# A three-stage transformer kernel: another slot order, smaller tiles and half-size broadcasts in its cross-attention

## The reference, cut to what matters

```
xn = _ln(x, lnx_g, lnx_b)            # 256 x 128
yn = _ln(y, lny_g, lny_b)            # 64 x 64, the context
q = jnp.einsum('bsc,hcd->bhsd', xn, wq)
k = jnp.einsum('btc,hcd->bhtd', yn, wk)
v = jnp.einsum('btc,hcd->bhtd', yn, wv)
a = jax.nn.softmax(jnp.einsum('bhsd,bhtd->bhst', q, k) * D ** (-0.5), axis=-1)
o = jnp.einsum('bhst,bhtd->bhsd', a, v)
x_out = x + o @ li1_w + li1_b
```

## Time and profile before

| what | us |
|---|---|
| median of 3 runs | 1399.13 (1396.72 to 1405.87) |
| the profiled execution | 1397.05 |
| its span | 1395.2 |
| TensorE busy | 1307.3 (94% of the span) |
| VectorE busy | 980.1 (70%) |
| ScalarE busy | 853.1 (61%) |
| GpSimd busy | 663.5 (48%) |
| mean granted TensorE clock | 0.973 |

### The profile page before, as it was taken

The page is one execution under the profiler, slowest core; times in us unless marked ns, Lnnn a source line. Parts: engine busy times, 40 slices in busy tenths (PEclk is TensorE's granted clock), DMA queues, the critical chain, the costliest instruction groups (busy, mean ns, idle before and its releaser), DMA issues.

```text
span 1395.2 us, 44119 instructions
## 1 busy us (share of the span) xinstructions
PE 1307.3 (94%) x18510; PEld 850.3 (61%) x18510; DVE 980.1 (70%) x2242; ACT 853.1 (61%) x1349; POOL 663.5 (48%) x1139
## 2 busy tenths in 40 slices
PE   7899999998999998989999999998989999999895
PEld 4455555554455553556777777665767777677584
DVE  6788888875555554577888888754567887787343
ACT  3687777776656665567777777654446666542352
POOL 4455666532001003245766666452337777445265
PEclk6999999998999998999999999999999999999998
DMA  7000000000600000000000001002001111122451
GB/s 230 4 4 3 4 3 3 3 4 2 174 0 1 1 1 1 1 2 18 33 26 26 33 18 33 33 33 61 1 17 48 48 48 48 47 83 90 145 169 45
DMA packets 54884, 53.85 MB, mean 39 GB/s; under 512 B 8999, under 2 KB 48939, under 8 KB 54432
## 3 DMA queue, kind: packets, MB, share of 16 engines
q1 hardware_dynamic: 50784, 44.21, 10.4%
q0 software_dynamic: 2816, 6.11, 1.3%
q10 hardware_dynamic: 1088, 0.72, 0.3%
HBM read 20.35 MB, written 14.49 MB: 25 GB/s over the span
## 4 chain that ended last, share of the span: by engine, by line
PE 77%; DVE 11%; POOL 4%; ACT 3%; issue 3%; DMA 1%; SPq 1%; POOLq 0%; DVEq 0%; ACTq 0%
PE psum L1574 6%; PE psum L1602 4%; DVE a_nm L623 4%; PE psum L960 4%; PE psum L962 4%; PE psum L961 4%; PE psum L1234 4%; PE psum L1198 3%; PE psum L2641 3%; PE psum L381 2%; PE psum L535 2%; PE psum L1545 2%; PE psum L1586 2%; PE psum L2062 2%; PE psum L2071 2%
## 5 line engine op out<-in xcount | busy, mean ns | idle before, releaser
L1657 DVE TENSOR_REDUCE b_nm<-psum 128x4 f16<-128x1024 f32 x128 | 156.6, 1223 | 52.2 <-PE psum L1579 51.5
L740 ACT ACTIVATE a_prob<-psum 128x768 f32<-128x768 f32 (+1 forms) x160 | 136.1, 853 | 50.5 <-PE psum L467 48.8
L623 DVE TENSOR_REDUCE a_nm<-psum 128x4 f16<-128x1024 f32 (+1 forms) x96 | 117.3, 1222 | 26.3 <-PE psum L480 25.1
L792 POOL TENSOR_SCALAR_AFFINE_SELECT a_prob<-a_prob 128x512 f32<-128x512 f32 x128 | 84.3, 659 | 106.4 <-ACT a_prob L740 106.3
L171 POOL TENSOR_TENSOR f_ln_rstd<-f_ln_tmp,pow_half 128x4 f32<-128x4 f32 x24 | 25.4, 1058 | 199.6 <-DVE f_ln_tmp L160 199.5
L1088 ACT ACTIVATE xo_sb<-psum,f_w_h_s 128x512 f32<-128x512 f32 x64 | 44.0, 688 | 88.3 <-PE psum L962 88.3
L1574 PE MATMUL psum<-b_QTh,b_KTh 32*128 32x256 f16 x512 | 70.4, 273 | 7.3 <-DVE b_nm L1657 5.2
L1579 PE MATMUL psum<-b_KTh,b_QTh 32*128 32x256 f16 x512 | 70.7, 273 | 1.2 <-DVE b_nm L1657 1.2
L1574 PE MATMUL psum<-b_QTh,b_KTl 32*128 32x256 f16 x512 | 69.4, 268 | 0.0
L1574 PE MATMUL psum<-b_QTl,b_KTh 32*128 32x256 f16 x512 | 69.3, 268 | 0.0
L1579 PE MATMUL psum<-b_KTl,b_QTh 32*128 32x256 f16 x512 | 69.3, 268 | 0.0
(11 more groups left out here) (462 smaller groups left out, 4623.2 us busy)
## 6 DMA issues: line engine op xcount, KB each, us to landing
f_h_wh<-b_rden SPq DMA_DIRECT2D x64, 128.0 KB, 2.1
f_h_wh<-c_rden SPq DMA_DIRECT2D x64, 128.0 KB, 2.1
expert_in<-empty SPq DMA_DIRECT2D x8, 662.5 KB, 11.4
m_xt<-expert_in SPq DMA_DIRECT2D x7, 662.5 KB, 4.9
m_w<-in_L_ffn_w_dram SPq DMA_DIRECT2D x16, 256.0 KB
x_sb<-in_x_dram SPq DMA_DIRECT2D x8, 256.0 KB, 4.5
f_w_h_w<-in_L_ffn_h_w_dram SPq DMA_DIRECT2D x2, 1024.0 KB, 7.7
out_dram<-m_send SPq DMA_DIRECT2D x8, 256.0 KB, 2.4
```

What stands on the lines that cost most here:

```text
L623: nc.vector.tensor_reduce(out, psum[:, banks, :].rearrange("p i (a b) -> p i a b", a=groups), X, ALU.max, negate=True).then_inc(max_done, 1)
L740: nc.scalar.activation(prob[unit % 5][:, :, 0:width], psum[:, first:first + 2, 0:width], ACT.Exp, scale=SCALE).then_inc(exp_done, 1)
L792: nc.gpsimd.affine_select(out=diagonal, in_=diagonal, compare_op=ALU.is_ge, fill=0.0, base=0, pattern=[[0, 4], [1, P]], channel_multiplier ...
L1657: v.tensor_reduce(self.nm[:, :, :].rearrange("p t (j r) -> p j t r", r=32)[:, 2 * e:2 * e + 2, :, g], self.pr.psum[:, 2:4, :].rearrange("p ...
```

## The change

- **Order.** New slots. Both score groups stand in a row (slots 0 and 1), values at 2 and 4, the maxima of the next batch at 3 (behind the second exponential, which still reads the banks), then `o`, `nm`, `k`, `q0`, `q1`. On VectorE `rden` moves to slot 5 and `vector_scaled` to slot 9. ScalarE drains the values before the projections.
- **Maxima** are made from the high halves alone: 32 products instead of 96.
- **Values** use 64 x 32 tiles: for each e eight products, one for each of 4 head positions and each half of the keys, into two banks (4 and 5). The weight tile holds no zeros any more. One activation copies V.
- **Sums** are made once per batch, 16 products with 128 x 32 tiles and 128 columns each, into columns 256 to 383 of bank 4. They come out as 128 x 128, so the reciprocal has 128 elements per partition instead of 256.
- **Broadcast**: 8 DMAs per batch of 64 KB each instead of 4 of 128 KB.
- `k` and `v` have their halves padded to 128 rows with zeros.
- `tensor_values` of batch n at e = 0 still waits for `rden` of n - 1. `vector_rden` waits for `num_out` too, since it reads the bank that ScalarE reads.
- **Router bias**: its weights are loaded in the stage before (class `Gate`), and GpSimd prepares the rows at the start of the last feed-forward.
- The rows of `li1_w` are reordered outside the kernel to fit the new order of heads.

```diff
-    SLOT = {"z": -11, "k": -8, "q0": -7, "q1": -6, "v": -4, "nm": -1, "o": 14}
-    SCORES, VALUES, MAXIMA = {0: 0, 1: 2}, {0: 3, 1: 5}, -4
-    FIRST, LAST = -23, 8 * (B - 1) + 17
+    SLOT = {"v": -7, "z": -13, "o": 13, "nm": -2, "k": -10, "q0": -9, "q1": -9}
+    COPIED = {**SLOT, "v": -6}
+    SCORES, VALUES, MAXIMA, FIRST_MAXIMA = {0: 0, 1: 1}, {0: 2, 1: 4}, -5, -4
+    BANKS = (4, 5)
+    FIRST, LAST = -25, 8 * (B - 1) + 17
...
             for i in range(2):
-                for (x, y) in ((0, 0), (0, 1), (1, 0)):
-                    for j in range(4):
...
+                for j in range(4):
...
-        for i in range(2):
-            for pair in range(2):
-                g = 2 * e + i
-                t.matmul(psum[TC * pair:TC * pair + TC, 6, 0:T], self.group_col[:, g, :, :].rearrange("p a d -> p (a d)"),
-                         prob[:, pair, i * T:i * T + T], start=(g == 0), stop=(g == self.G - 1), skip_group_check=True)
...
+        for b in range(4):
+            for a in range(2):
+                keys = slice(TC * a, TC * a + TC)
+                inst = t.matmul(psum[D * b:D * b + D, self.BANKS[a], 0:T], self.V[n % 2][keys, 2 * (2 * e + b % 2) + b // 2, :],
+                                prob[keys, b // 2, b % 2 * T:b % 2 * T + T], start=True, stop=True, skip_group_check=True)
+        if e == 1:
+            inst = self.tensor_sums(n)
         inst.then_inc(self.av_done, 1)
+
+    def tensor_sums(self, n):
+
+        for e in range(2):
+            prob = self.prob[(2 * n + e) % 3]
+            for h in range(2):
+                for b in range(4):
+                    first = b % 2 * T + h * P
+                    inst = self.nc.tensor.matmul(self.pr.psum[self.D * b:self.D * b + self.D, self.BANKS[0], T:T + P],
+                                                 self.chosen[:, e, h, :], prob[:, b // 2, first:first + P], start=False,
+                                                 stop=(e + h == 2), skip_group_check=True)
+        return inst
...
         if n:
-            v.wait_ge(self.rb_there, 64 * n)
-        v.reciprocal(self.rden[:, :], self.pr.psum[:, 6, 0:T]).then_inc(self.rden_done, 1)
+            v.wait_ge(self.rb_there, 128 * n)
+        v.wait_ge(self.num_out, 2 * (n + 1))
+        v.reciprocal(self.rden[:, :], self.pr.psum[:, self.BANKS[0], T:T + P]).then_inc(self.rden_done, 1)
...
     def vector_slot(self, s):
-        for _, n in self.parts(s, {0: self.MAXIMA}):
+        for n in self.maxima_at(s):
             self.vector_max(n)
         for use in self.parts(s, self.SLOT):
             if use[0][0] in "qk":
                 self.vector_low(use)
-        for _, n in self.parts(s, {0: 6}):
+        for _, n in self.parts(s, {0: 5}):
             self.vector_rden(n)
-        for _, n in self.parts(s, {0: 11}):
+        for _, n in self.parts(s, {0: 9}):
             self.vector_scaled(n)
...
-        for k, n in self.parts(s, {4: -13, 0: -23, 1: -21, 2: -18, 3: -16}):
+        for k, n in self.parts(s, {4: -18, 0: -25, 1: -23, 2: -20, 3: -20}):
             self.vector_normed(n, k)
...
     def gpsimd_slot(self, s):
-        for _, n in self.parts(s, {0: -11}):
+        for _, n in self.parts(s, {0: -13}):
             self.gpsimd_low(n)
+        for _, n in self.parts(s, {0: -24}):
+            self.ln_in.gpsimd_rstd(n)
         for _, n in self.parts(s, {0: -22}):
-            self.ln_in.gpsimd_rstd(n)
-        for _, n in self.parts(s, {0: -20}):
             self.gpsimd_unnormed(n)
-        for _, n in self.parts(s, {0: -17}):
+        for _, n in self.parts(s, {0: -19}):
             self.ln_c.gpsimd_rstd(n)
-        for _, n in self.parts(s, {0: -15}):
             self.ln_x.gpsimd_rstd(n)
-        for _, n in self.parts(s, {0: 16}):
+        for _, n in self.parts(s, {0: 15}):
             self.gpsimd_output(n)
...
             for g in range(self.G):
-                y.dma_start(self.rb[:, g, :], self.rden[g:P:4, :].unsqueeze(1).to_broadcast([P // 4, 4, T])).then_inc(
-                    self.rb_there, 16)
+                for h in range(2):
+                    y.dma_start(self.rb[:, g, h * P:h * P + P],
+                                self.rden[2 * g + h:P:8, :].unsqueeze(1).to_broadcast([P // 8, 8, P])).then_inc(self.rb_there, 16)
...
-            if n == 2 and routing:
-                routing.gpsimd_bias()
...
+                    gate.start()
...
+        self.gate.gpsimd_halves()
```

More of the change, by code:

```diff
@@ L1884, in __init__ @@
         self.zi = sb("zi", [P, 2, C])
[L1885 to L1888, removed]
+        self.zT, self.cT = ([sb(f"{x}T{k}", [P, cols], F32 if k == "w" else F16) for k in "whl"]
+                            for x, cols in (("z", T), ("c", P)))
+        self.halves = {x: [sb(f"{x}{half}", [P, HID], F16) for half in "hl"] for x in ("wq", "wk", "wv")}
         self.QT = [[sb(f"QT{half}{i}", [P, G, T], F16) for half in "hl"] for i in H2]
         self.KT = [[sb(f"KT{half}{i}", [P, G, TC], F16) for half in "hl"] for i in H2]
-        self.V = [sb(f"V{i}", [P, H // 2, 2, self.D]) for i in H2]
+        self.V = [sb(f"V{i}", [P, H // 2, self.D]) for i in H2]
         self.nm = sb("nm", [P, 2, P], F16)
@@ L1921, in bank_of @@
     def bank_of(self, use):
-        return self.pr.psum[:, (5, 7)[self.ring.slot(use)], :]
+        return self.pr.psum[:, (6, 7)[self.ring.slot(use)], :]
     def tokens(self, m, n):
@@ L1928, in row2, with maxima_at @@
         return self.w[name][:, :].unsqueeze(1).to_broadcast([P, 2, C])
+    def maxima_at(self, s):
+        if s == self.FIRST_MAXIMA:
+            return [0]
+        return [n for _, n in self.parts(s, {0: self.MAXIMA}) if n]
     def vector_prepare(self):
-        v, G, done = self.nc.vector, self.G, self.prepared
+        v, G, done, low = self.nc.vector, self.G, self.prepared, slice(CC, P)
         v.memset(self.nm[:, :, :], 0.0)
-        for m in self.V:
-            v.memset(m[...], 0.0)
-        v.memset(self.group_col[...], 0.0).then_inc(done, 1)
+        for m in (*self.cT[1:3], *self.halves["wk"], *self.halves["wv"]):
+            v.memset(m[low, :], 0.0)
+        v.memset(self.chosen[...], 0.0).then_inc(done, 1)
         v.tensor_reduce(self.group[:, :], self.pr.ident[:, :].rearrange("p (j r) -> p r j", r=32)[:, 0:G, :], X,
@@ L1951, in gpsimd_split @@
             self.w.arrived(g)
-        g.tensor_copy(high[:, :], self.w[x][:, :]).then_inc(self.split_high, 1)
+        rows = slice(0, P if x == "wq" else CC)
+        g.tensor_copy(high[rows, :], self.w[x][:, :]).then_inc(self.split_high, 1)
         g.wait_ge(self.split_high, i + 1)
-        g.tensor_tensor(low[:, :], self.w[x][:, :], high[:, :], ALU.subtract).then_inc(self.split_low, 1)
+        g.tensor_tensor(low[rows, :], self.w[x][:, :], high[rows, :], ALU.subtract).then_inc(self.split_low, 1)
     def tensor_drained(self, use):
@@ L2218, in scalar_slot @@
             self.scalar_scores(n, e)
[L2219 removed]
+        for e, n in self.parts(s, self.VALUES):
+            self.scalar_values(n, e)
+        for use in self.parts(s, self.COPIED):
             self.scalar_projection(use)
[L2221 to L2222 removed]
     def gpsimd_unnormed(self, n):
@@ L2237, in gpsimd_low @@
             g.wait_ge(self.pro_full, self.ring.full(("v", n - 1)))
-        for whole, high, low in (self.cT, self.zT):
-            inst = g.tensor_tensor(low[:, :], whole[:, :], high[:, :], ALU.subtract)
+        for (whole, high, low), rows in ((self.cT, slice(0, CC)), (self.zT, slice(0, P))):
+            inst = g.tensor_tensor(low[rows, :], whole[rows, :], high[rows, :], ALU.subtract)
         inst.then_inc(self.z_low, 1)
@@ L2859, in layout @@
             a[k] = np.ascontiguousarray(v.reshape(*v.shape[:-1], 4, 4, -1).swapaxes(-3, -2).reshape(v.shape))
+        elif k == "L1_xattn_a2_li1_w":
+            heads = [(2 * e + b % 2) * 4 + 2 * (b // 2) + i for e in range(2) for i in range(2) for b in range(4)]
+            a[k] = by_chunk(v.reshape(H, -1, C)[heads].reshape(v.shape))
         elif k.endswith(("li1_w", "li3_w", "li2_b")):
```

104 lines of the change are left out of this document (51 added, 53 removed).

## The result

The changed kernel takes 1422.64 us (median of 4 runs, 1421.41 to 1429.44), the kernel before 1397.93 beside it: ratio 1.0191 [1.0159, 1.0224]. The forecast was 1413 in 1385 to 1430. The direction and the mechanism came out; the loss is 25 us where the sum said 14.4. The profiled execution is 1421.97 us, its span 1420.2, 25.0 more than before.

| part | before | after | measured | predicted |
|---|---|---|---|---|
| up to the first reciprocal's end | 1034.0 | 1031.9 | -2.1 | -0.5 |
| 15 turns | 175.7 | 201.2 | **+25.5** | +15.8 |
| from the last reciprocal's end | 185.5 | 187.1 | +1.6 | -0.9 |

What follows compares the result with a forecast made beforehand. PE bounds the kernel before; after, VectorE's reciprocal-broadcast-scaling loop binds. Turns of 182.8 plus long issues 8.7 make 191.5 (+15.8); head -0.5, tail +0.6, router bias -1.5 give +14.4, said as 1413 us, range 1385 to 1430.

Steps and rivals of the forecast that it cites:

- PE's demand: PE's own work per cross-attention batch, claimed to fall from 11.7 to about 9.4 us.
- The loop binds: VectorE's loop from reciprocal through broadcast, scaling and maxima to the next reciprocal sets the batch: 12.6 us against 11.74.
- rival B: The loop binds but long issues are rare or hidden: 12.6 us per batch, 1405 us; chance 0.28.
- 6.62 us from the reciprocal to the scaling: Broadcast term of the loop: 4.04 us now plus 2.58 for four more DMA issues on SyncE.
- 5.98 from the scaling to the next reciprocal: VectorE's rest of the loop: scaling 1.14, `zi` 0.52, maxima 2.26, statistics 0.39 and 0.76, reciprocal 0.91 us.
- Long issues, +0.58: Instruction loads starting inside SyncE's burst of eight broadcasts lengthen an issue: 0.58 us more per batch, 13.2 in all.
- the landing: Time from a broadcast DMA's issue to its landing, 2.1 us, left unchanged within the broadcast term.
- Head: The part up to the first reciprocal's end: -0.5 us, with 2 either way.
- Tail: After the last reciprocal: +0.6 us for the feed-forward starting behind `o` of batch 14, -1.5 for the router bias wait.
- Rival C: PE, idle in lumps, drops to half clock; 14 us a batch, 1425 us; chance 0.1.
- Rival A: The broadcast does not bind: 11.2 us a batch with long issues, 1383 us, or 1370 at the floor; chance 0.22.
- So PE sets the pace: Kernel before, cross-attention: PE busy 11.73 of 11.74 us a batch, VectorE and GpSimd close behind.

Runs made afterwards that it cites:

- run 1: The changed kernel with four of its eight broadcast DMAs per batch left out, so the output differs; 1384.06 us, ratio 0.99 to the kernel before.
- run 2: The kernel before with each of its four broadcasts per batch cut into two of 64 KB, nothing else changed; 1429.35 us, ratio 1.0248.
- run 4: The changed kernel with VectorE's scaling two slots later (11 for 9), behind the maxima; 1433.54 us, ratio 1.0205 to the kernel before.
- Run 8: The kernel before with the maxima made from the high halves alone (32 products a batch instead of 96); 1405.83 us, ratio 0.9999.
- run 9: The changed kernel with five of eight broadcasts on SyncE and three on ScalarE; 1408.93 us, ratio 1.003 to the kernel before.
- run 5: The changed kernel with six broadcasts on SyncE, two on ScalarE: 1404.12 us, ratio 1.0002; with the scaling two slots later as well: 1434.01 us, 1.0206.
- run 7: The changed kernel, scaling two slots later, `o` behind k, statistics for `zi` earlier: 1410.25 us, 1.0017; also with six/two broadcasts on SyncE/ScalarE: 1411.16 us, 1.0047.

## Why the prediction was right, and where its sum was short

- **PE's demand** (9.4 us): close. Values 0.66 for 0.6, sums 1.08 for 1.0, maxima 0.41 for 0.37; at full clock PE is busy for 9.75 to 9.77 us in five turns and for 10.27 in three (as in the turn shown above). It had no weight while the loop stood at 12.6.
- **The loop binds**: right, in 15 of 15 turns, with 57.8 us of waiting for the DMA, and runs 1 and 2 show it from both sides. The forecast's mechanism holds, and rival B (few long issues) is out with 13 of them. That 1% is about what a measurement tells from no change was too cautious: the interval here is 0.3% to either side.
- **6.62 us from the reciprocal to the scaling**: 6.50 undisturbed. The 2.58 for four more issues fits (5.03 for 2.46). From the last issue's end to the scaling it takes 1.44 with 64 KB and 1.55 with 128. By the cost that the Trainium skill, "DMA: Bandwidth & Descriptors", section Anatomy of one DMA, gives for GpSimd's path, that difference would be 0.15, an estimate, and the trace, of SyncE's DMAs, comes near it (0.11).
- **5.98 from the scaling to the next reciprocal**: 5.85.
- **Long issues, +0.58**: 0.61. Right.
- **The term that failed is the landing.** "From issue to landing 2.1 us, of which I leave all" took the median as if it were constant. It is 2.0 without an instruction load behind the last issue, and about 2.9 to 3.8 with one: +0.84 a turn, 12.6 us. With -1.8 and -1.6 from the first two terms above and +0.5 from the long issues that makes the 9.7 by which the turns exceed 191.5. That the total came within the forecast's own 1404 to 1424 is in part luck: without the two terms that were too long the turns would have missed by 13.1. I also took loads as evenly spread. Of 25, 20 start between the first issue and the scaling, in 59% of the time. PE, which runs k, q, the scores and the values just then and idles before the scaling, consumes its instructions there; that this is the reason was argued, not tested.
- **Head**: -2.1 for -0.5, inside the 2 either way.
- **Tail**: +1.6 for -0.9. The first feed-forward's transposes start 1.6 us after the last reciprocal, as foreseen behind `o` of batch 14; but this `o` took 3.51 us, not 1.95. PE's timeline, with the router's first wait, and the busy time of the stretch of `o`:

```profile
1231.35 3.51 PE L2019 MATMUL psum<-c_w_li,f_h_wl 128*128 128x128 f32 x16 [4.47 <-DVE f_h_wl L2169]
1234.70 0.60 PE L1220 MATMUL psum<-ident,b_w_wq 128*128 128x128 f32 x4
...
1262.18 0.18 PE L2552 MATMUL psum<-m_hot,m_earlier 128*128 128x32 f16 x1 [0.68 <-DVE m_carry L2500]
```
```profile
1231.10:1234.50 3.40, 3.15 (x15) 3.18 (x16) 3.27 (x15) 0.00 (x0) 0.00 (x0) 0.50 0.03 9
```

  After 4.47 us without work PE ran at 0.50, the 1.2 GHz level, 1.6 us more than the same product took before. The wait of 1.46 us for the router's bias is gone, but 4 us later PE now waits 0.68 us for VectorE, where it did not before, and of the 1.5 forecast some 0.8 are gained. These two make 2.3 of the 2.5 us by which the tail is over.
- **Rival C**, the clock: it exists (0.95 over the stage, five stretches of 3.4 us at half clock in it) and costs nothing in the turns, since the loop has no product in it: 5.85 stays in those batches too. In this kernel it costs only where nothing hides it, 1.6 in the tail; in run 4, where `o` is in the loop, it costs in the turns too.
- **Rival A**: not what happened, but its price was near. For a broadcast of 4.8 us it had 11.2 a turn and 1383 us, 16 below the kernel before; run 1, with 4.76, has 10.9 and is 12 below. By the Trainium skill, "TensorEngine Tiling (Array Packing)", section PSUM Bottleneck, the copies out of PSUM may be next. With the broadcast halved VectorE leads the chain that ended last (its maxima, which it reads from PSUM, have 20.9%), but 23% of it are still broadcast, and a turn is 10.7 us where VectorE's own chain was put at 10.3. Run 1, 1062 to 1170 us:

```profile
by line: DVE c_nm L2132 20.9%; DMA f_h_wh<-c_rden 14.3%; issue 9.1%; SPq L2289 8.6%; DVE c_z L188 5.5%; DVE c_zi L188 4.9%; DVE c_QTl L2145 4.4%; DVE c_rden L2161 4.4%; POOL c_lni_rstd L171 4.4%; POOL c_lnx_rstd L171 2.9%; POOL c_lni_tmp L1
```

- **"So PE sets the pace" before**: read too strongly. Run 8 cuts PE by 0.7 us a batch and gains nothing, and in the trace of before the scaling already waits for the DMA in 10 of 15 turns, 0.16 to 1.51 us. It changed nothing in this sum, because the loop I added was longer than both.

## What to carry to other kernels

When a change halves an engine's work by splitting a transfer, count issues, not bytes: eight DMAs of 64 KB cost 2.6 us more than four of 128 KB, and they stood in a loop in which nothing could hide them. Price a DMA in a loop by its distribution, not by its median: the one late landing in the trace of before was a sample of the term that this sum missed. And before moving an instruction out of one loop, follow who stands behind it on the other engines; the later scaling took 2.2 us out of its own loop and made another of 13.7, which moving `o` behind k only shortened.

## What the hardware showed that was not expected

- Loads of instructions for PE (16 KB, 0.9 to 1.6 us, one per 8 us of this stage) disturb a broadcast in both halves of its life: one issue takes up to 1.85 us instead of 0.60, or the landing is 0.9 to 1.8 us late. That the late packets stand behind the load on their DMA engine is likely, not shown.
- Issues on SyncE and ScalarE run side by side: six and two were through in 4.1 us in undisturbed batches, though ScalarE began 1.2 us late, where eight on one queue took 5.02. ScalarE's first issue begins while its copy before it still runs (1084.90 against 1084.84, run 9).
- The scaling, same operands and shape, took 1.23 us in the changed kernel and 1.80 in run 4. GpSimd's work as such does not slow it: beside its rstds (`c_lni_rstd`, `c_lnx_rstd`), as in the kernel before, it stays at 1.22 to 1.24. But in all 50 scalings of runs 4, 5 and 7 that run beside GpSimd's forming of `c_zTl`, the low half of the tokens, it takes 1.52 to 2.11, the longer the more they overlap. What in this instruction slows it was not isolated.
